# Values of all heads by seven block products ahead of the loop, and a loop one step deeper

## The reference, cut to what matters

```python
B, LQ, LK, D, H, DH = (8, 128, 128, 512, 32, 128)
x   = rmsnorm(hidden) * ln_weight
h_q = (x @ w_q.T).reshape(b, lq, H, DH)
h_k = (key_value @ w_k.T).reshape(b, lk, H, DH)
h_v = (key_value @ w_v.T).reshape(b, lk, H, DH)
score = einsum('bqhd,bkhd->bhqk', h_q, h_k) + position_bias
score = softmax(where(mask, score, -inf)), 0 where masked
out = einsum('bhqk,bkhd->bqhd', score, h_v).reshape(b, lq, H*DH) @ w_out.T
return hidden + out
```

## Time and profile before

| | us |
|---|---|
| median of 3 executions | 1042.22 (1042.18 to 1042.51) |
| profiled execution, its own time | 1042.18 |
| its span, first to last instruction | 1040.4 |
| TensorE busy | 1011.1 |
| VectorE busy | 718.3 |
| ScalarE busy | 505.4 |
| GpSimd busy | 463.1 |

### The profile page before, as it was taken

The page is one execution under the profiler, slowest core; times in us unless marked ns, Lnnn a source line. Parts: engine busy times, 40 slices in busy tenths (PEclk is TensorE's granted clock), DMA queues, the critical chain, the costliest instruction groups (busy, mean ns, idle before and its releaser), DMA issues.

```text
span 1040.4 us, 17490 instructions
## 1 busy us (share of the span) xinstructions
PE 1011.1 (97%) x5856; PEld 885.6 (85%) x5856; DVE 718.3 (69%) x1310; ACT 505.4 (49%) x1223; POOL 463.1 (45%) x402
## 2 busy tenths in 40 slices
PE   8999999999999999999999999999999999799995
PEld 7887888888899998989899998989999897578784
DVE  6768767577767777676777777676767767663615
ACT  7745444555545545455454554554545545343251
POOL 0345775454535435255353453544535434352204
PEclk9999999999999999999999999999999999899997
DMA  7533544422121120211212112212022130300011
GB/s 263 185 140 125 180 163 152 172 94 94 27 93 63 43 93 25 93 63 55 81 35 83 63 55 81 65 54 89 30 89 67 43 114 22 112 20 1 1 41 41
DMA packets 39140, 86.07 MB, mean 83 GB/s; under 512 B 5184, under 2 KB 9280, under 8 KB 39104
## 3 DMA queue, kind: packets, MB, share of 16 engines
q1 hardware_dynamic: 39104, 85.62, 24.4%
HBM read 66.73 MB, written 18.87 MB: 82 GB/s over the span
## 4 chain that ended last, share of the span: by engine, by line
PE 87%; DVE 5%; POOL 3%; ACT 2%; issue 2%; DMA 1%; SPq 0%; DVEq 0%; POOLq 0%; ACTq 0%
PE psum L1656 25%; PE psum L1658 24%; PE psum L1657 24%; PE psum L1662 8%; PE psum L1663 3%; PE psum L1826 3%; DMA raw<-in_dft 1%; POOL cx_lo L768 1%; ACT smx L1026 1%; POOL mix L614 0%; POOL stat L760 0%; POOL stat L758 0%; DVE xn_lo L1226 0%; DVE rsum L1565 0%; DVE acc L1507 0%
## 5 line engine op out<-in xcount | busy, mean ns | idle before, releaser
L614 POOL TENSOR_TENSOR mix<-kf,mix 128x512 fp32r<-128x512 f32 x64 | 113.8, 1778 | 144.6 <-ACT mix L824 144.6
L665 POOL TENSOR_TENSOR smx<-far,bias 128x512 f32<-128x512 f32 x64 | 83.1, 1299 | 173.0 <-DVE smx L1318 172.3
L1656 PE MATMUL psum<-wvq_lo,cx_hi 128*128 128x256 f32 x512 | 149.6, 292 | 0.0
L1658 PE MATMUL psum<-wvq_hi,cx_hi 128*128 128x256 f32 x512 | 144.9, 283 | 0.0
L1657 PE MATMUL psum<-wvq_hi,cx_lo 128*128 128x256 f32 x512 | 144.8, 283 | 0.0
L1026 ACT ACTIVATE smx<-smx,nmax 128x128 f32<-128x128 f32 x256 | 99.7, 390 | 82.8 <-DVE nmax L1324 82.8
L824 ACT ACTIVATE av_hi<-psum 128x512 fp32r<-128x512 f32 x140 | 83.8, 599 | 105.5 <-PE psum L1663 66.7
L1656 PE MATMUL psum<-mix,av_hi 128*128 128x512 f32 x256 | 105.9, 414 | 1.0 <-issue 1.0
L1656 PE MATMUL psum<-xn_lo,wvq_hi 128*128 128x512 f32 x272 | 106.1, 390 | 0.0
L1657 PE MATMUL psum<-xn_hi,wvq_lo 128*128 128x512 f32 x272 | 105.9, 389 | 0.0
L1658 PE MATMUL psum<-xn_hi,wvq_hi 128*128 128x512 f32 x272 | 105.9, 389 | 0.0
(11 more groups left out here) (222 smaller groups left out, 2634.7 us busy)
## 6 DMA issues: line engine op xcount, KB each, us to landing
kf<-k_blocks SPq DMA_DIRECT2D x64, 256.0 KB, 2.6
raw<-in_wk SPq DMA_DIRECT2D x16, 512.0 KB, 3.6
k_blocks<-far SPq DMA_DIRECT2D x32, 256.0 KB, 2.3
raw<-in_wv SPq DMA_DIRECT2D x16, 512.0 KB, 4.9
raw<-in_wq SPq DMA_DIRECT2D x16, 512.0 KB, 3.5
raw<-in_wo SPq DMA_DIRECT2D x16, 512.0 KB, 3.4
raw<-in_ffn SPq DMA_DIRECT2D x10, 512.0 KB, 3.8
k_blocks<-rest SPq DMA_DIRECT2D x16, 256.0 KB, 2.0
```

The source lines that it names most:

```text
L614: g.tensor_tensor(dst_lo, src, dst_hi, ALU.subtract).then_inc(s_lo, 1)
L665: nc.gpsimd.tensor_tensor(bm, far[:, HB * hf:HB * hf + HB, :], g_, ALU.add).then_inc(s_bm_ready, 1)
L1656: mm(out, lhs(0), rhs(1), start=first, stop=False)
L1658: return mm(out, lhs(0), rhs(0), start=False, stop=last)
```

## The change

1. The values of all heads are projected ahead of the loop by block products as well: `GROUPS` = 32, groups 1 to 15 are the key pairs as before, groups 16 to 31 are values. A set of seven value weight blocks (from two loaded pieces) covers two pairs of heads and serves two groups, one for each half of the tiles, so weights are formed in odd groups only. A block product is 12 matmuls of 256 columns with the context as the loaded operand. The blocks of V are stored to memory (`v_blocks`).
2. The loop has no `values`. Each unit loads a block of V (`load_v`), rounds it on ScalarE (`v_hi`) and takes its rest on GpSimd (`v_lo`).
3. The loop is one step deeper: `project(n+2)`, `turn_probs(n)`, `outputs(n-3)`, `attend(n)`, `scores(n+2)`; VectorE handles `attended(n-1)` in unit n.
4. The softmax works in place in one of two buffers, `soft[parity]`.
5. The wq weights move from `wvq` to `ext`. The first two `UP` weights are loaded and split in the first pair, the other two in the last pair, all on GpSimd.

```diff
+V0_PIECE = K0_PIECE + PAIRS
+QUADS = PAIRS // 2
+GROUPS = PAIRS + 2 * QUADS
+K_SETS = PAIRS - 1
...
-        scores_sb, exps, probs, bm = (smx[:, i] for i in range(4))
+        soft, bm = (smx[:, 0], smx[:, 1]), smx[:, 3]
...
+        def next_set(p):
+            if p < PAIRS:
+                return p
+            return set_of(p) + 1 if p % 2 and p + 1 < GROUPS else None
...
+            def load_v(g, j):
+                if is_first(g):
+                    sp.wait_ge(s_kp_mm, BLOCKS * (GROUPS - 2) + 4)
+                    sp.wait_ge(s_kst[C11 if j < 2 else C12], 16 * (PAIRS + 2))
+                else:
+                    sp.wait_ge(s_v_lo, 4 * g + (j - 3))
+                    for i in range(4):
+                        sp.wait_ge(s_kst[i], 16 * GROUPS)
+                sp.dma_start(vf_row(j), row(vd, 4 * g + j)).then_inc(s_vf[j], 16)
...
             def pair_pool(g):
...
-                    if not (last and j == 3):
-                        bias_and_mask(n + 1, *nxt(g, j))
-                        k_lo(n + 1, *nxt(g, j))
+                    if not (last and j >= 2):
+                        g2, j2 = after(g, j, 2)
+                        k_lo(n + 2, j2)
+                        v_lo(n + 2, j2)
+                        bias_and_mask(n + 2, g2, j2)
                     if j == 1 and not last:
                         wq_lo(g + 1, 0)
-                        wv_lo(g + 1)
                     if j == 2:
-                        wo_lo(g)
                         if not last:
                             wq_lo(g + 1, 1)
+                        wo_lo(g)
+                    if (is_first(g) or last) and j in (1, 3):
+                        split_low(UP[j // 2 + (2 if last else 0)])
...
             def pair_act(g):
...
+                    if not (is_first(g) and j == 0):
+                        attended_hi(n - 1, 8 * g - 4 + (4 if j == 3 else -4 if j == 0 else 0) + (0 if j else 4), prev(j))
+                    if not (last and j >= 2):
+                        k_hi(n + 2, *after(g, j, 2))
+                        if due(n - j % 2):
+                            act.wait_ge(s_a_mm, n - j % 2)
+                        v_hi(n + 2, *after(g, j, 2))
...
+                    if not (last and j >= 2):
+                        q_hi(n + 2, psQ)
+                    if due(n):
+                        act.wait_ge(s_a_mm, n)
+                    hi_of(s_t_mm, s_t_hi, n + 1, flat(pt[0]), psT[:, :])
+                    if not (last and j == 3):
+                        exps_of(n + 1, (j + 1) % 2)
+                    if j == 2:
+                        if due(8 * g):
+                            act.wait_ge(s_o_mm, 8 * g)
+                        wo_hi(g)
...
-            def softmax_in(n):
+            def softmax_in(n, parity):
+                s = soft[parity]
                 dve.wait_ge(s_scores_mm, n + 1)
                 dve.wait_ge(s_bm_ready, n + 1)
                 if due(4 * n):
                     dve.wait_ge(s_exp_done, 4 * n)
+                if due(n - 1):
+                    dve.wait_ge(s_t_mm, n - 1)
...
             def pair_dve(g):
...
+                    softmax_in(n + 1, (j + 1) % 2)
+                    if last and j == 2:
+                        probs_lo(n)
+                    if not (is_first(g) and j == 0):
+                        attended(n - 1, prev(j))
+                    if not (last and j == 2):
+                        probs_lo(n)
+                        lo_of(s_q_hi, s_q_lo, n + 3, qk[1][:, 0], psQ[:, :], qk[0][:, 0])
+                    has_out = not (is_first(g) and j < 3)
+                    if has_out:
+                        add_out(n - 3, 0, 2 * ((j + 1) % 4))
+                    softmax_out(n + 1, (j + 1) % 2)
+                    if has_out:
+                        add_out(n - 3, 1, 2 * ((j + 1) % 4) + 1)
...
-            def k_product(p, block):
+            def product(p, block):
...
+                else:
+                    for b in range(2):
+                        tk = slice((2 * (p % 2) + b) * P, (2 * (p % 2) + b + 1) * P)
+                        for c in range(2):
+                            last = mm3(out[:, 2 * P * b:2 * P * (b + 1)], lambda i: rows_of(i, c)[:, tk],
+                                       lambda i: weights_of(i, w, block)[:, c, :], c == 0, c == 1)
...
-            for p in range(1, PAIRS):
-                k_pair_pe(p)
+            for p in range(1, GROUPS):
+                if p == GROUPS - 1:
+                    project(0, 0, 0, banks[4])
+                group_pe(p)
...
+            project(1, 0, 1, banks[5])
             scores(0)
-            values(2, 0, 4, 0)
-            values(2, 0, 4, 1)
+            project(2, 0, 2, psQ)
+            scores(1)
...
-                    if more:
-                        values(n + 2, g + (j >= 2), (2 * j + 4) % B, 0)
-                    turn_probs(n)
-                    if more:
-                        values(n + 2, g + (j >= 2), (2 * j + 4) % B, 1)
-                    if front:
-                        scores(n + 1)
-                    attend(n, g, j)
-                    if not (isinstance(g, int) and (g == 0 and j < 2 or last and j == 3)):
-                        outputs(n - 2, g - (j < 2), (2 * j + 4) % B)
+                    turn_probs(n, j % 2)
+                    if not (is_first(g) and j < 3):
+                        outputs(n - 3, g - (j < 3), 2 * ((j + 1) % 4))
+                    attend(n, g, j)
+                    if front:
+                        scores(n + 2)
```

More of the change, by code:

```diff
@@ L358, in build, with staged, vf_row, after @@
         kf32 = kf.bitcast(F32)
-        staged = {C22: flat(smx[:, 3]), C21: flat(far[:, 0:HB]), C12: flat(far[:, HB:B]),
-                  C11: flat(rest)}
+        def staged(p, i):
+            if i == C22:
+                return flat(smx[:, 3])
+            if i == C11:
+                return flat(rest)
+            if p < PAIRS:
+                return flat(far[:, 0:HB]) if i == C21 else flat(far[:, HB:B])
+            return rows[:, 0 if i == C21 else 1]
         def kf_row(j):
             return kf32[:, j * HALF:(j + 1) * HALF]
+        def vf_row(j):
+            return wvq[0].bitcast(F32)[:, j * HALF:(j + 1) * HALF]
+        def after(g, j, by):
+            return (g, j + by) if j + by < 4 else (g + 1, j + by - 4)
+        def prev(j):
+            return (j + 3) % 4
         def nxt(g, j):
@@ L539, in _ @@
                     load(k_piece(p + SLOTS), t["wk"][p + SLOTS])
-                elif p == 12:
-                    k_consumed(12)
-                    load_wv(0)
-                elif p == 13:
-                    k_consumed(13)
-                    load_wq(0)
+                elif p < PAIRS:
+                    load(V0_PIECE + p + SLOTS - PAIRS, t["wv"][p + SLOTS - PAIRS])
+                elif p % 2 == 0 and p + SLOTS < GROUPS:
+                    for pair in (p + SLOTS - PAIRS, p + SLOTS + 1 - PAIRS):
+                        load(V0_PIECE + pair, t["wv"][pair])
+                elif p == GROUPS - 4:
+                    load_wq(0)
+                if p == PAIRS:
+                    for j in range(4):
+                        load_k(0, j)
+            store_block(GROUPS - 1, C22)
+            store_block(GROUPS - 1, C11)
             for j in range(4):
-                load_block(0, j)
-            for i in (C22, C11, C21, C12):
-                store_block(PAIRS - 1, i)
+                load_v(0, j)
+            store_block(GROUPS - 1, C21)
+            store_block(GROUPS - 1, C12)
             def pair_loads(g):
@@ L588, in load_ffn @@
                 sp.dma_start(raw[:, ffn_slot(k), 0:src.shape[1]], src).then_inc(s_landed[ffn_slot(k)], 16)
-            for k in range(FFN_PIECES):
+            every_pair(sp, pair_loads)
+            for i in (C21, C12):
+                sp.wait_ge(s_kst[i], 16 * GROUPS)
+            sp.dma_start(rows[:, 0], t["gamma"].partition_broadcast(P)).then_inc(s_rows_landed, 16)
+            sp.dma_start(rows[:, 1], t["beta"].partition_broadcast(P)).then_inc(s_rows_landed, 16)
+            for k in range(FC1, FFN_PIECES):
                 load_ffn(k)
@@ new lines, in last_sum, with group_pool @@
+            def last_sum(w):
+                pool.wait_ge(s_ks_plo, 3 * w + 2)
+                pool.wait_ge(s_s_sum, 4 * w + 3)
+                g.tensor_tensor(part(w, S4), part(w, A12), part(w, S2), ALU.subtract).then_inc(s_s_sum, 1)
+            def group_pool(p):
+                w = next_set(p)
+                if w is not None:
+                    if p < PAIRS:
+                        first_sums(w)
+                    if not is_v(w):
+                        second_sum(w)
+                    weights_lo(w, A11)
+                elif p % 2 == 0:
+                    first_sums(set_of(p) + 1)
@@ L1600, in _ @@
             x2_lo(1)
-            ffn_lo(UP[3])
             for i in range(2):
```

545 lines of the change are left out of this document (266 added, 279 removed).

## The result

The changed kernel takes **1130.08 us** (median of 4 runs, 1128.74 to 1131.8) against 1042.29 us of the kernel before, timed beside it: 1.0843 times as long, 95% interval 1.0824 to 1.0862. The forecast was 1026.5 us, range 1018 to 1037. It was wrong in sign and by 104 us.

What follows compares the result with a forecast made beforehand. TensorE, busy 97% of 1040.4 us, was taken as the bound; 1042.2 - 23.0 + 8.9 + 2.4 - 4.2 + 0.5 = 1026.8, say 1026.5 us. The range was 1018 to 1037 us.

Steps and rivals of the forecast that it cites:

- timetable of a loop unit: In the loop: VectorE's 7.2 us and its waits fit a unit of 7.70 us, so the loop stays TensorE's.
- Rival D: In the loop VectorE becomes the bound, waiting twice per unit for ScalarE's copies: 55 us more, 1081; chance 0.06.
- Value matmuls, -23.0: Values by block products: 1344 matmuls instead of 1536, 192 fewer at 0.120 us each, -23.0 us.
- The groups ahead of the loop: New value groups: VectorE's and GpSimd's work fits beside TensorE's 10.1 us per group, margin 0.6 us, cost nothing.
- rival B: GpSimd and VectorE hold each other up in odd groups ahead of the loop, up to 1.3 us each: 1037; chance 0.14.
- +0.5: Conversion of K to V weights in group 15, where ScalarE also doubles rows: +0.5 us, bounds 0 and 2.
- Start, +8.9 and +2.4: Start of the loop: TensorE idle 10.9 us less 2.0 of before, +8.9; clock falling to 1.2 GHz, +2.4.
- End, -4.2: End of the loop: up-weight splits moved away, wo_lo put on the path; idle 12.1 before, 7.8 after; bounds -8 and 0.
- half clock after that idle 3.5 us: End of the loop: reason given beside the bounds -8 and 0 of the end's saving.
- Rival C: The end gains nothing, since the wo chain and a fall of the clock replace the splits: 1031; chance 0.10.
- Rival A: Start of the loop: no fall of the clock, 2.4 less, and better covered, 3 less: 1021; chance 0.17.

Runs made afterwards that it cites:

- experiment 1: The changed kernel with ScalarE's wait ahead of `attended_hi` in each pair's first unit asking for 8g-6 output steps instead of 8g-4: 1035.42 us, ratio 0.9936.
- experiment 5: The changed kernel with 14 further matmuls of 128x512 per pair in TensorE's pause, in the 14 middle pairs: 1091.31 us, ratio 1.0471.
- experiment 3: The changed kernel with the same kind of over-wait also in each pair's third unit, 8g instead of 8g-4: 1221.59 us, ratio 1.172.
- Experiment 8: The kernel of experiment 1 plus one VectorE addition of 128x512 in each of 56 units: 1043.96 us, median of 10, ratio 0.999.
- experiment 6: Three kernels on experiment 1: another GpSimd order ahead of the loop, 1032.12 us; four changes at the loop's end, 1031.38 us; both, 1029.88 us.
- experiment 2: The changed kernel with 8g-5 instead of 8g-4 in ScalarE's wait in each pair's first unit: 1082.23 us, ratio 1.0409.
- experiment 7: Waits before GpSimd's long subtractions, added to experiment 6's kernel with both changes: in the first pair 1027.49 us, in the last 1026.11 us, both 1024.07 us.

## Why the prediction was wrong

**The step that failed** is the timetable of a loop unit: "`softmax_in` 0.2 to 2.4, `attended` to 3.75, then the transposes' copy, which ScalarE has ready at 4.05", with the conclusion "on time by over 1 us". It was worked out from durations and from the order of each queue. It took every wait of ScalarE as a wait for its own operand. The count ahead of `attended_hi` was never put in for j = 0, 1, 2 and 3; done, it says 8g-4 at j = 0, which TensorE reaches only 6 us into the unit (714.5 to 720.5), and the copy of the probabilities then comes at 723.4. A term of +95 us was missing: 52 of pauses (15 x 3.50) and 43 of half clock. Experiments 1 and 5 measure the whole (94.7) and its clock part (38.8 in 14 pairs); experiment 3 adds 91.5 by a second over-wait, in other shares.

**Rival D** had the right engines (VectorE waiting for ScalarE's copies in order), but the wrong reason: not a queue that is too full, but a wait on TensorE's own later work. The corrected count leaves VectorE's work untouched and the loop is TensorE's. That the price of D, 1081, lay on the right side is no merit of it. In experiment 1 VectorE's busy time is 7.58 us per unit (155.5 of 160), above the 7.2 of the forecast, but about 0.8 of it is `nmax` held up by GpSimd. Experiment 8 shows that room.

**The terms that can be judged with the wait corrected** (1035.4, 8.9 us over the forecast):

- Value matmuls, -23.0: the block products run without a gap (240 to 280). A unit takes 7.80 us, and 10.66 - 24 x 0.120 = 7.78, so the 7.70 took 0.08 too much off: the 1.52 us of the second half of `values` hold the slower first matmul behind the transposes (0.20 us to the next start), which stays. The term itself was right to 0.02 us a unit, 1.2 in all.
- The groups ahead of the loop, 0 with bounds of 1.3 per odd group (rival B): TensorE has no wait in the value groups. The group that holds K's last and V's first sums cost two waits, 1.11 and 0.17 us (at 202.72 and 204.52), against +0.5.
- Start, +8.9 and +2.4: from 366 to 410, in experiment 1, TensorE is idle for 10.3 us and the stretches at 0.50 to 0.74 cost another 3.9, 14.2 in all where 13.3 had been priced before the 2.0 of the old start were taken off. Mechanism and sum were right; of the parts, the idle time came out lower than priced (10.9) and the clock higher (2.4).
- End, -4.2: mis-sized. Idle time of 6.8 us and half clock of 5.7 make 12.5, where 7.8 was forecast and 12.1 stood before. The wait for wo (1.95) was there; but the bound "half clock after that idle 3.5 us" was left in the range and not in the sum, and the scaling that GpSimd held up (2.77 for 0.69) was not foreseen. **Rival C** was right here.
- Together 1.2 + 0.8 + 0.9 + 4.7 = 7.6 of the 8.9 us, and 0.3 had been rounded off. Of the last 1.0, 0.66 is a wait of `attend` at 418.14, behind that window; the rest was not traced.

**Rival B** named the right mechanism at the wrong place. It costs TensorE nothing in the block products, and VectorE 2 us at each of three places at the ends of the loop, where GpSimd's instruction is 128x1024 and long.

**Rival A**, no fall of the clock and a start shorter by 3 us, did not happen in the changed kernel. A start shorter by 3.3 us was to be had by GpSimd's other order (experiment 6).

**The chance.** Faster had 0.93. With the count corrected it is faster (0.9936), and tuned at the ends it reaches 1024.1, better than the forecast. But what was to be forecast was the kernel with its count, and slower had 0.06, all of it rival D's.

## What to carry to other kernels

When a change shifts a loop by a step, put the numbers into every semaphore count for every value of the loop's inner index, and note for each who reaches it and when in the unit. A wait that is too strict changes no result, only the time; and what it costs is set by the queue behind it, twice over when the engine it starves lies idle long enough for its clock to fall. In the trace, follow the releasers to the engine with the longest idle time (here TensorE 3.50, VectorE 4.19, ScalarE 8.45): the cause stands there, not at the name in TensorE's list of waits.

## What the runs showed of the hardware that was not expected

- Equal pauses of TensorE, 2.12 us in the same place of the loop, are followed by half clock in some pairs and by full clock in others (experiment 2: six of 15), while pauses of 3.50 us were followed by it in all 15. In the changed kernel the stretch at 0.50 behind a pause (724 to 729) was longer than the pause. Matmuls whose results nobody reads kept it at 1.00 (experiment 5).
- A VectorE instruction on 4 columns (`nmax`, 128x4, one tensor input) took 2.15 us beside a GpSimd subtraction of 128x1024, and 0.95 on average in the loop, against 0.17 when free. All 58 held rows of experiment 1 from 410 us on and all 16 of the kernel before end with the GpSimd instruction under which they started. The held time is shown as busy: VectorE reads 97% busy in experiment 1 (155.5 of 160 us), and from 600 to 800 us experiment 8 put 0.60 us more work into each unit while `nmax` shrank by 0.55.
- One added VectorE operation per unit made a kernel whose runs spread over 12 us (experiment 8), where the kernels of experiments 1, 6 and 7 spread over 1 to 3. The kernel of experiment 2 spread over 11, with its mean clock.
